# Where the split maxima are turned inside a round of a perceiver kernel: behind the scores, or behind the next maxima

## The reference, cut to what matters

```python
q = _split_heads(query @ Wq.T + bq)
k = _split_heads(bank @ Wk.T + bk)       # bank: 32 x 1601 x 256
v = _split_heads(bank @ Wv.T + bv)
scores = jnp.einsum('bhqd,bhkd->bhqk', q / score_scale, k)
attn = jax.nn.softmax(scores, axis=-1)   # the maximum of each row is subtracted
ctx = jnp.einsum('bhqk,bhkd->bhqd', attn, v)
```

## Time and profile before

| what | value |
|---|---|
| median of 3 runs | 2135.73 us (2132.75 to 2143.18) |
| the profiled execution's own time | 2127.42 us |
| span of the profiled execution | 2125.6 us |
| mean granted TensorE clock | 0.986 |
| PE busy | 1970.4 us (93%) |
| DVE busy | 1327.1 us (62%) |
| ACT busy | 1049.7 us (49%) |
| POOL busy | 615.0 us (29%) |

### The profile page before, as it was taken

One profiled execution on the slowest core, in us unless ns is written; L12 is line 12 of the kernel. 1 busy time (PEld: TensorE's weight loads), 2 busy tenths in 40 slices (PEclk: granted clock), 3 DMA queues, 4 the chain that ended last, 5 costly groups with the idle time before them and its releaser, 6 DMA issues.

```text
span 2125.6 us, 72645 instructions
## 1 busy us (share of the span) xinstructions
PE 1970.4 (93%) x31796; PEld 1585.3 (75%) x31796; DVE 1327.1 (62%) x2500; ACT 1049.7 (49%) x1532; POOL 615.0 (29%) x998
## 2 busy tenths in 40 slices
PE   5789999999999999999999989999999998999987
PEld 4677777777778787787878778787777776777764
DVE  2656656856656666666666585665666666566644
ACT  3354455555465555455555544555545444434442
POOL 3222323323233232333324222332323222122201
PEclk7999999999999999999999999999999999999999
DMA  5533434343433333434333424243342321213122
GB/s 181 180 119 107 155 128 133 112 136 116 133 118 109 114 137 116 139 108 144 122 111 129 143 76 160 92 154 100 107 147 84 121 70 61 77 50 107 50 71 70
DMA packets 124471, 243.91 MB, mean 115 GB/s; under 512 B 13952, under 2 KB 44800, under 8 KB 124160
## 3 DMA queue, kind: packets, MB, share of 16 engines
q1 hardware_dynamic: 123568, 239.23, 34.1%
q10 hardware_dynamic: 592, 0.04, 0.0%
HBM read 235.94 MB, written 3.15 MB: 112 GB/s over the span
## 4 chain that ended last, share of the span: by engine, by line
PE 73%; DVE 13%; ACT 7%; issue 5%; POOL 1%; DMA 0%; SPq 0%; DVEq 0%; POOLq 0%; ACTq 0%
PE M L805 11%; PE M L812 11%; PE SC L1023 9%; PE SC L1046 8%; PE O L1067 7%; PE X L862 5%; ACT probT L1269 4%; DVE mx L1614 4%; PE SC L1039 3%; PE M L862 3%; PE X L1133 2%; PE M L906 1%; PE X L1107 1%; PE M L867 1%; PE X L841 1%
## 5 line engine op out<-in xcount | busy, mean ns | idle before, releaser
L1614 DVE TENSOR_REDUCE mx<-SC 128x4 f32<-128x1600 f32 (+1 forms) x256 | 466.6, 1823 | 138.1 <-PE SC L1023 134.7
L1269 ACT ACTIVATE probT<-SC 128x2048 f32<-128x2048 f32 (+1 forms) x256 | 398.7, 1557 | 165.9 <-PE SC L1046 165.4
L654 POOL TENSOR_TENSOR rowsT<-raw,rowsT 128x384 fp32r<-128x384 f32 (+1 forms) x256 | 280.0, 1115 | 394.9 <-ACT rowsT L1323 394.8
L812 PE MATMUL M<-wvs,rowsT 128*128 128x256 f32 x2496 | 359.4, 293 | 2.7 <-ACT kT L1208 1.4
L805 PE MATMUL M<-rowsT,wks 128*128 128x400 f32 (+1 forms) x1536 | 341.1, 362 | 11.3 <-DVE V L1415 4.4
L1208 ACT ACTIVATE kT<-M,bk 128x400 f32<-128x400 f32 (+1 forms) x256 | 151.6, 594 | 380.3 <-PE M L805 379.8
L805 PEld LDWEIGHTS M<-rowsT,wks 128*128 128x128 f32 x1536 | 269.8, 190 | 85.9 <-issue 64.0
L812 PEld LDWEIGHTS M<-wvs,rowsT 128*128 128x128 f32 x2496 | 315.9, 192 | 23.1 <-issue 3.3
L1415 DVE TENSOR_TENSOR V<-M,bv 128x256 f32<-128x256 f32 (+1 forms) x448 | 159.5, 397 | 276.6 <-PE M L812 265.9
L1023 PE MATMUL SC<-kT,bdq 32*128 32x400 f32 (+1 forms) x2048 | 245.1, 547 | 26.6 <-ACT probT L1269 22.5
L1067 PEld LDWEIGHTS O<-probT,V 128*17 128x17 f32 x13312 | 193.9, 99 | 79.9 <-issue 75.2
(11 more groups left out here) (275 smaller groups left out, 2456.5 us busy)
## 6 DMA issues: line engine op xcount, KB each, us to landing
ring<-in_ws_dram SPq DMA_DIRECT2D x428, 256.0 KB, 4.4
summed<-in_ctx_dram SPq DMA_DIRECT2D x60, 800.5 KB, 4.5
raw<-in_ctx_dram SPq DMA_DIRECT2D x64, 384.0 KB, 4.7
raw<-in_ctx_dram SPq DMA_DIRECT2D x32, 512.0 KB, 4.3
ring<-rounded_scratch SPq DMA_DIRECT2D x64, 256.0 KB, 3.9
raw<-in_ctx_dram SPq DMA_DIRECT2D x32, 321.0 KB, 4.6
out_dram<-x SPq DMA_DIRECT2D x16, 128.0 KB, 2.3
kT<-in_ctx_dram SPq DMA_DIRECT2D x2, 800.5 KB, 8.8
```

What stands on the lines that cost most here:

```text
L654: pool.tensor_tensor(rowsT[1][:, c, at], raw[:, c, at], rowsT[0][:, c, at], ALU.subtract).then_inc(low_ready, 1)
L812: mm = pe.matmul(bank[:, (t - 2 * a) * D:(t - 2 * a + 1) * D], rowsT[xp][:, cc, t * P:(t + 1) * P], wvs[wp][:, cc, :], start=(at == cc == ...
L1269: act.activation(probT[step % 3][0:w, :, 0:len(ts), :].rearrange("p j t q -> p j (t q)"), SC[0:w, :, 0:len(ts) * P], ACT.Exp)\
L1614: dve.tensor_reduce(mx[c][:, :, n], SC[:, :, 0:KCH[n][1]], AX.X, ALU.max).then_inc(max_used, 1)
```

## The change

The two turns of the split maxima (`max1` in round k = 3, `max0` in round k = 7) move from place "A" to place "C" on all engines that walk the list: from right behind the scores to behind the maxima and the weighing of the round, in front of the key fills of "second". Their numbers in the order of `X` follow. Within "C", they stand ahead of `out`.

```diff
     if place == "B" and k == 1 and 0 < b < B:
         yield "sums", b - 1
-    if place == "A":
+    if place == "C":
         if k == 3 and 0 <= b < B:
             yield "max1", b
         if k == 7 and 0 <= b + 1 < B:
             yield "max0", b + 1
-    if place == "C":
         if b == B and k == 0:
             yield "sums", b - 1
         if k == (1 if b == B else 3) and 0 <= b - 1 < B and (b - 1) % 2:
             yield "out", b - 1
```

## The result

The changed kernel took 2156.51 us in the median of 4 runs (2153.76 to 2163.64), the kernel before 2134.24 us in 4 runs beside it (2131.55 to 2143.18). The ratio is 1.0101, with a 95% interval of 1.0083 to 1.0119: slower by 1%, 18 to 25 us. The forecast was 19 us more, 2154.5 us, with a range of 2143 to 2163.

What follows compares the result with a forecast made beforehand. The prediction took TensorE, busy for 93% of the span, as the bound; 9.0 + 1.6 + 2.2 + 4.6 + 0.8 + 2.6 = 20.8 us, less 2, gave +19 us, 2154.5 us, range 2143 to 2163.

Steps and rivals of the forecast that it cites:

- Given-back waits and the old chain: TensorE's 45.3 us of waits on DVE and ACT: 2 us taken off; rival with a quarter gone, 2145.5 us, chance 0.15.
- The turn itself, and the exponential: Turn on TensorE: 0.04 us saved, 0.04 paid; exponential on ACT 0.34 us earlier but hidden by the value fill: zero.
- Term 1: Round k = 3, even batches 2 to 30: `out` behind the turn starts 0.60 us late, 15 times, 9.0 us.
- Term 2: Round k = 7, odd batches: the turn waits for the GELU of `up0`, 0.15 us in 11 rounds, 1.6 us.
- Term 3: Late GELUs ahead of the turn: b = 17 1.0 us net, b = 7 and 21 0.6 each, together 2.2 us.
- Term 4: Late `ff_in` or `gru_in` copies: 1.6 us in b = 11 and 14, 1.3 in b = 3; together 4.6 us.
- Term 5: TensorE's granted clock falls behind the stalls in b = 3 and b = 17: two falls of 1.3, 2.6 us.
- the point named last in the prediction: Scores of k = 4 and k = 0 beginning to wait for `mT`: a sign the prediction is wrong, counted at nothing.
- The reason given against further falls: Clock stayed at 1.00 behind a 2.03 us wait; used against the rival of more clock falls, 2182 us, chance 0.02.

Runs made afterwards that it cites:

- the second profiles: The kernel before and the changed kernel, each unaltered, profiled once more; spans of 2133.1 us and 2156.9 us.
- The exchange on ACT alone: Against the kernel before: turns stay at A, ACT takes the exponential ahead of the copy to `mT`; ratio 1.000 (0.998 to 1.002).
- the control with `out` at D: Against the kernel before: turns stay at A, only `out` of round k = 3 moves from C to D, behind the key fill; ratio 1.0011.

## Why the prediction was right

*Given-back waits and the old chain.* Right: 45.3 us of waits on DVE and ACT before and 44.2 after, and 44.9 and 43.0 in the second profiles. That is 1.1 and 1.9 less, where 2 us were taken off. What two odd rounds give back was in the terms.

*The turn itself, and the exponential.* Both were counted at nothing. The exchange on ACT alone confirms the second, to within some 4 us. The first was not tried alone; but of the 30 rounds where `ff_in` or `gru_in` stands ahead of the turn, 22 kept their length to within 0.15 us: the copies were done in time, as forecast, and the turn between maxima and key fill cost nothing that shows.

*Term 1, `out`.* Forecast 15 x 0.60 = 9.0. The rounds are longer by 15 x 0.57 = 8.6 us, plus 0.9 in b = 18, where ACT did not answer at once, as the prediction had it do in all 15. The kernel with these rounds alone shows the waits in the trace and a loss of 6 to 15 us.

*Term 2, ordinary odd rounds.* Forecast 0.15 each; measured 0.15 to 0.17 in six, 0.23 and 0.25 in two, at most 0.02 in three.

*Term 3, late GELUs.* b = 7 and 21: 0.33 and 0.35, forecast 0.6 each. b = 17: 4.56 longer, fall of the clock included, and 2.41 shorter in the following round: 2.2, against 1.0 and a fall of 1.3.

*Term 4, late copies.* b = 11: 1.85; b = 14: 1.90, forecast 1.6 each; the turns wait 1.52 us in both. Here the wait is the evidence and not the length of the round: that of b = 11 is 1.99 us longer in the second profile of the kernel before as well, by a fall of the clock. b = 3: 2.8 with its fall, against 1.3 + 1.3. In b = 31 the 0.6 is not seen apart from the spread of that round.

*Term 5, the clock.* The mechanism held for the waits of about 3 us, and was too narrow in its scope. The sum allowed for two falls behind those two waits. It missed the start: the turn of batch 0 has no key fill behind it, the first scores wait 0.46 us for `mT`, and the clock of the first rounds is held down for 17 to 20 us. This is the point named last in the prediction (scores that wait for `mT`, counted at nothing), and it holds for one turn of 64. In the two pairs of traces it is worth 4.8 and 3.9 us; in the whole time that share could not be resolved.

The reason given against further falls, that the wait of 2.03 us left the clock at 1.00, does not carry either: in the control with `out` at D a wait of 2.03 us in the same round was followed by 0.50. The Trainium skill, TensorE: Matmul & The Clock Gate, section "HAM oscillation — how this bites in real kernels", tells of long waits between groups of matmuls, behind each of which the next group starts at the low clock. The traces agree for the waits of 3.0 to 3.3 us, with the clock at 0.50 at all 14 of them. The section does not speak of waits as short as those of `out`. In the first profile of the changed kernel the clock fell in none of the 15 rounds with `out`, in the second in one (b = 6).

*The account as a whole.* In the first pair of traces the rounds of terms 1 to 4, with the two falls, are 20.5 us longer, the start 4.8 and the end behind the last scores 1.3, of 26.4 us of span. In the second pair it is 18.9, 3.9 and 0.9, of 23.8. So the rounds that were named came out at or just under the sum of 20.8, and the start came on top. The clock as a whole is the least certain part: the time at 0.50 within the span went from 57 to 93 us in the first pair and from 77 to 96 in the second. TensorE was busy in 29 and 15 of these added us; at most half of that is lost, so by this estimate up to 15 and up to 7 us, against 2.6 forecast with an upper bound of 6.4. Part of it can be chance: the two profiles of the kernel before differ by 20 us at 0.50 and by 7.5 us of span.

The sum of 19 us is inside the measured 18 to 25. How the 3 us between forecast and median divide between the start and other falls of the clock stays open, since both vary from one execution to the next.

## What to carry to other kernels

When a small step on a shared buffer is moved, list its neighbours in that buffer at the new place, on both sides, with the end of the drain in front and the start of the fill behind; each pair without other work between them costs a full turn, copy and release (here 0.57 us each), and what stood between them before was worth its place. Then walk the same list for the first and the last pass of the loop, where the work that covers the step may be missing. And the gain that such a move seems to offer can be had alone, by exchanging only the other engine's two steps; here that showed a gain of nothing, to within some 4 us.

## What the runs showed of the hardware

A wait of TensorE of about 2 us in the same place (b = 3, turns at A) was followed by a fall of the granted clock to 0.50 in three of six profiles, behind 1.83, 1.99 and 2.03 us, and not behind 1.54, 1.74 and 2.03. At the 3.0 us of b = 17 it fell in seven of seven profiles. A wait of only 0.46 us at the start, in a stretch where TensorE was busy for 70 to 76% with it or without it, went with 17 to 20.5 us at 0.50 in six of six, against 0 to 7 us in the eight without it. So one execution's falls say little of a kernel, and the length of the wait alone did not decide them.
